# Expert layer 2: the softmax exponential of the router as a power on GpSimd, the ranking of experts two to three tiles later

## What is computed

```python
ln2_out = _layernorm(hidden_after_attn, ln2_weight, ln2_bias)
x = ln2_out.reshape(-1, H)
logits = jnp.einsum('th,eh->te', x, router_weight)          # 8 experts
gate = jax.nn.softmax(logits, axis=-1)
top_probs, top_idx = jax.lax.top_k(gate, TOP_K)             # 2 of 8
h_mid = jax.nn.gelu(jnp.einsum('th,ehf->etf', x, moe_w1))   # 128 -> 256
expert_out = jnp.einsum('etf,efh->eth', h_mid, moe_w2)      # 256 -> 128
weights = jnp.sum(jnp.where(top_idx[None] == e_ids, top_probs[None], 0.0), axis=-1)
moe_out = jnp.einsum('eth,et->th', expert_out, weights)
return hidden_after_attn + moe_out
```

## Time and profile before

| | |
|---|---|
| median of 3 runs | 976.86 us (973.74 to 979.7) |
| the profiled execution | 979.73 us |
| its span, first to last instruction | 978.0 us |
| TensorE matmul busy | 783.1 us, 80% |
| VectorE busy | 689.6 us, 71% |
| ScalarE busy | 429.1 us, 44% |
| GpSimd busy | 220.6 us, 23% |
| mean granted TensorE clock | 0.907 |

### The profile page before, as it was taken

One profiled execution on the slowest core, in us unless ns is written; L12 is line 12 of the kernel. 1 busy time (PEld: TensorE's weight loads), 2 busy tenths in 40 slices (PEclk: granted clock), 3 DMA queues, 4 the chain that ended last, 5 costly groups with the idle time before them and its releaser, 6 DMA issues. The chain is left out here.

```text
span 978.0 us, 28213 instructions
## 1 busy us (share of the span) xinstructions
PE 783.1 (80%) x10948; PEld 595.1 (61%) x10948; DVE 689.6 (71%) x1882; ACT 429.1 (44%) x848; POOL 220.6 (23%) x369
## 2 busy tenths in 40 slices
PE   2579888887338999999999716887875899999998
PEld 1345555554236777777777513655654688888886
DVE  4578888875547888888888537887753666666653
ACT  2122222221215666666666415665642455555553
POOL 4333333330430111111110086543200111111100
PEclk9568889999758999999999958999996899999999
DMA  3000000510100000010010000000000000000000
GB/s 91 20 19 20 19 19 11 128 27 11 22 7 18 27 26 27 26 27 27 26 27 27 18 0 2 5 4 4 4 4 2 1 12 11 11 11 11 9 11 14
DMA packets 31381, 19.20 MB, mean 20 GB/s; under 512 B 10590, under 2 KB 29740, under 8 KB 31276
## 3 DMA queue, kind: packets, MB, share of 16 engines
q1 hardware_dynamic: 28236, 16.73, 6.7%
q10 hardware_dynamic: 3040, 0.98, 0.4%
HBM read 7.22 MB, written 2.10 MB: 10 GB/s over the span
## 5 line engine op out<-in xcount | busy, mean ns | idle before, releaser
L1734 PEld LDWEIGHTS bank<-w2r,hme 128*128 128x128 f32 x1024 | 132.2, 191 | 16.3 <-ACT hme L1575 2.1
L1734 PE MATMUL bank<-w2r,hme 128*128 128x128 f32 x1024 | 135.6, 276 | 0.5 <-DVE Xq L1677 0.5
L1575 ACT ACTIVATE hme<-bank,b 128x512 f32<-128x512 f32 x128 | 86.4, 687 | 96.0 <-PE bank L97 95.9
L833 DVE TENSOR_SCALAR bank<-bank 128x512 f32<-128x512 f32 x128 | 88.9, 695 | 28.7 <-PE bank L904 28.7
L1677 DVE SCALAR_TENSOR_TENSOR Xq<-bank,wgte,Xq 128x128 f32 (+1 forms) x256 | 72.1, 344 | 51.1 <-PE bank L1734 38.1
L754 ACT ACTIVATE P<-bank 128x512 f32<-128x512 f32 x128 | 76.7, 599 | 66.6 <-PE bank L913 66.4
L841 DVE TENSOR_REDUCE mx<-bank 128x4 f32<-128x512 f32 x128 | 87.1, 681 | 2.1 <-PE bank L896 2.1
L350 ACT ACTIVATE sg<-bank 128x512 f32<-128x512 f32 x40 | 23.9, 597 | 127.8 <-PE bank L581 94.0
L913 PE MATMUL bank<-mT,negsel 128*128 128x128 f16 x512 | 50.1, 220 | 16.8 <-DVE bank L833 12.7
L896 PE MATMUL bank<-K,Q 128*128 128x128 f16 x512 | 51.1, 224 | 11.9 <-issue 6.5
L728 POOL TENSOR_TENSOR inv_sum<-inv_sum,dn 128x16 f32<-128x16 f32 x32 | 7.0, 220 | 230.4 <-DVE dn L872 230.4
(11 more groups left out here) (387 smaller groups left out, 2076.0 us busy)
## 6 DMA issues: line engine op xcount, KB each, us to landing
K<-Kc SPq DMA_DIRECT2D x128, 32.0 KB, 1.8
X<-in_x SPq DMA_DIRECT2D x8, 256.0 KB, 2.9
Xq<-X SPq DMA_DIRECT2D x32, 64.0 KB
Yq<-Y SPq DMA_DIRECT2D x32, 64.0 KB
out_x<-Xq SPq DMA_DIRECT2D x32, 64.0 KB, 1.7
cload<-in_ctx SPq DMA_DIRECT2D x8, 192.0 KB, 2.6
w1r<-in_L_ffn_moe_w SPq DMA_DIRECT2D x1, 1024.0 KB
w_raw<-in_L_ffn_w_gate ACTq DMA_DIRECT2D x1, 256.0 KB, 3.3
```

The lines of the kernel that those rows point to most:

```text
L833: dve.tensor_scalar(TB[j % 2][:], TB[j % 2][:], -CLIP, CLIP, ALU.max, ALU.min).then_inc(s["t_clip"], 1)
L1575: act.activation(hm[:, p % HR], UP[p % RING][:], ACT.Gelu_apprx_tanh, bias=b1[:, p:p + 1]).then_inc(s["gelu"], 1)
L1734: last = pe.matmul(Y[e % 2][:, cols], hm[:, p % HR, cols], w2r[:, p], start=(p % 2 == 0 and i == 0), stop=(p % 2 == 1), skip_group_check=True)
```

## The change

The exponential of the router moves from ScalarE to GpSimd, as a power with base e, from a new constant tile `euler`. GpSimd's residual addition goes from p = 9 to p = 5, in front of it. VectorE's three later pieces go from p = 11, 12, 13 and 14 to p = 13, 14 and 15, the last two of them joined.

```diff
+        euler = sb("euler", [128, GB, NE])
 ...
             @block.gpsimd
                 pool.memset(half[:], -0.5)
+                pool.memset(euler[:], 2.718281828459045)
 ...
-                        if nxt(g) and p == 9:
+                        if nxt(g) and p == 5:
                             pool.tensor_tensor(xg(X3, g + 1), xg(X3, g + 1), xg(H, g + 1), ALU.add
                                                ).then_inc(s["r_ready"], 1)
+                        if nxt(g) and p == 10:
+                            pool.wait_ge(s["g_in"], g + 2)
+                            pool.tensor_tensor(pr[:], euler[:], lg[:], ALU.pow).then_inc(s["g_exp"], 1)
 ...
             @block.scalar
-                        if nxt(g) and p == 10:
-                            act.wait_ge(s["g_in"], g + 2)
-                            act.activation(pr[:].rearrange("p b e -> p (b e)"), lg[:].rearrange("p b e -> p (b e)"),
-                                           ACT.Exp).then_inc(s["g_exp"], 1)
 ...
             @block.vector
-                    elif p == 11:
+                    elif p == 13:
                         dve.wait_ge(s["g_exp"], g + 1)
 ...
-                    elif p == 12:
+                    elif p == 14:
                         other = pr[:].unsqueeze(2).broadcast_to(deep)
 ...
-                    elif p == 13:
+                    elif p == 15:
                         tie = before8[:].unsqueeze(1).broadcast_to(deep)
 ...
-                    elif p == 14:
                         link(g, dve.tensor_reduce(cnt[:], c8[:, 1], AX.X, ALU.add))
```

## The result

The changed kernel took 984.91 us (median of 12 runs, 981.48 to 989.52) against 979.37 us for the kernel before (12 runs, 973.74 to 985.4): ratio 1.0055, 95% interval 1.003 to 1.008, that is 5.4 us more, with an interval of 2.9 to 7.8. The forecast was 6.8 us more. The profiled execution took 985.67 us, with a span of 984.0.

The account below looks back on a forecast made before the run. TensorE was taken to bound the loop, and VectorE's chain the start. A 5.3 us pause, 1.5 us of lower clock and 0 for the loop made 6.8 us on a median of 976.86: 983.7 us, range 979.5 to 991.

Parts of the forecast that it names:

- What bounds the kernel: Expert stage: only TensorE's stream sets the loop's time; at the start the chain runs through the exponential and VectorE.
- The 2.1 us of weight loads: Downward product's weight loads waiting for ScalarE's gelu: taken as absorbed by the matmul queue, gain 0, at most 2.1 us.
- The price: GpSimd's new 32-element power: 5.44 us, from the -0.5 power of equal size; bounds 0.22 and 6.0 us.
- The line through the shorter powers: Upper bound on the GpSimd power's length, by the slope of the 4- and 8-element powers: 6.0 us.
- The start: In step(-1) VectorE's sum comes 5.27 us later, so TensorE stands still 5.3 us for the second group's xn.
- can't begin: Step(-1): VectorE can't begin the second group's preparation before finishing the first group's routing weights, so its delay delays the end.
- The clock: TensorE's clock falls to 1.2 GHz in the start's pause; 2.9 us at half speed lose 1.5, bounds 0 and 2.9.
- The loop: Inside the loop VectorE's pieces come 1.0 us later, 0.3 us of reserve remain before TensorE's product; cost 0.
- The rival of a stalled loop: TensorE waits at p = 4 each turn if the power costs 6 us or more; about 986 to 992, chance 0.22.
- The port: Rival: GpSimd's long power holds up VectorE's combine, near 3 us in each of 7 groups; about 1005, chance 0.04.
- the `combine` that the prediction set against it: Evidence against the port rival: combine at 820.97 took its usual 1.13 us over a GpSimd power of 1.02 us.
- The sum: Whole kernel: 5.3 + 1.5 + 0 = 6.8 us more, 983.7 us against the median of 976.86, +0.7%.

Follow-up runs that it names:

- e1: Changed kernel with only the first group's exponential back on ScalarE, the other seven still powers on GpSimd; ratio to the kernel before 0.9986.
- e5: Changed kernel with all eight exponentials on ScalarE, keeping VectorE's later ranking and GpSimd's addition at p = 5; ratio to the kernel before 1.0025.
- e2: Changed kernel with 20 unused matmuls on TensorE before its wait for the second group's xn, filling the pause; ratio to the kernel before 1.0053.
- e8: Changed kernel with the first group's ranking pieces moved behind the second group's statistics on VectorE, p = 15 behind xn; ratio to the kernel before 1.0011.
- e3: Changed kernel with VectorE's pieces left at p = 11, 12, 13 and 14 as before the change; ratio to the kernel before 1.0169.
- e4: e1 with an unused 4-element power on GpSimd in front of each of the seven powers; ratio to the kernel before 1.0041.
- e7: e1 with an unused 8-element power on GpSimd in front of each of the seven powers; ratio to the kernel before 1.0058.
- e9: e1 plus 12 filler matmuls in TensorE's first xn wait and first group's p = 15 behind second group's statistics; 976.03 us, ratio to kernel before 0.9959.

## Why the prediction was right, by its steps

**What bounds the kernel.** Right: TensorE in the loop, VectorE's chain at the start. e1 and e5 show it from both sides, since neither seven exponentials on ScalarE nor seven powers on GpSimd change a turn by 0.01 us. The 2.1 us of weight loads that waited for gelu were worth nothing.

**The price.** I took 5.44 us by the row of the same shape; measured 5437 to 5438 ns, all eight. The line through the shorter powers (6.0) would have been 0.6 too high. At this shape the power of e costs what that of -0.5 does (5439 ns). Of the 15 table loads one is left.

**The start.** Forecast 5.27 us; measured 5.25 at VectorE's sum and, by e2, 5.24 at TensorE. With e8 the reason is shown too: it is what stands behind the wait on VectorE. That VectorE "can't begin" the second group before it has finished the first group's weights was the order of its stream, and no need of the data: e8 begins it earlier.

**The clock.** The mechanism was right, the size small: forecast 1.5 us, from one rise, measured 1.94 in the changed kernel's profile (1.07 in e3's). This is the term that was mis-sized. The sum took half of 2.9 us, the unbroken work at 1.2 GHz at the stage's start. After the pause the clock was 0.50 from the first work at 777.52 until 782 to 783, some 5 us. The first 1.1 us of that, the transposes, cost nothing, because the product behind them starts as late with the pause filled (16.33 us behind the bias addition in e2, 16.32 here), where it waits for `Xq`; half of the other 4.0 is the term. The Trainium skill (TensorE: Matmul & The Clock Gate, Part 1) has an idle array put back to 1.2 GHz and 2.4 GHz given again only after sustained work; the fall to 0.50 within the idle stretch and the late rise agree with it. Timed runs could not show the term.

**The loop.** Forecast: pieces 1.0 us later and 0.3 us of reserve left, at no cost. Measured 1.0 us later, 26.17 us a turn, and a reserve of 0.42 (e4) and 0.41 (e7). The predicted reserve was 0.1 short; its use as a threshold held. The rival of a stalled loop would have come true with a power of over 5.9 us (5.44 + 0.42); e4, whose power ends as late as one of 6.4 us would, is that case, at 0.57 a turn.

**The port.** Out: `combine` takes 344 ns by the median and 352 at most in the changed kernel, where two of each turn (813.33 and 816.39) run beside a power, and in e8 addition, statistics and aggregation (0.69, 0.87, 0.38 us) run under it at their usual length. The Trainium skill's warning (GPSIMD Engine Reference, 8, Key points) speaks of VectorE's instructions in a two-port mode or with two inputs in SBUF. `combine` takes the bank from PSUM, so these rows don't test it, nor did the `combine` that the prediction set against it. In e8 an instruction with two inputs in SBUF runs beside GpSimd's root, also a power. It keeps its 0.19 us, and the same holds for the comparisons behind it:

```profile
766.98 1.01 POOL L1552 TENSOR_TENSOR rs<-rs,half 128x4 f32<-128x4 f32 x1
```

```profile
767.08 0.19 DVE L1621 TENSOR_TENSOR pr<-pr,r 128x32 f32<-128x32 f32 x1
```

**The sum.** 6.8 forecast, 7.18 by the profile's stage, 5.4 (2.9 to 7.8) by time. The difference between the last two is inside what timing can tell. The absolute 983.7 us came near the measured 984.91 with some luck: it stood on a median of 976.86 from three runs, which was 979.37 over twelve, so a start 2.5 us too low and an addition 1.4 us too high cancelled in part.

## To carry to other kernels

Price an operation that changes engine at the place where nothing covers it: in a loop with a hand-written order that is the first turn, where eight equal operations had one payer. Where an in-order engine waits longer for a new producer, look at what stands behind the wait and whether it needs the result; moving one addition and its statistics ahead of it took away three quarters of the loss (5.44 of 7.18 us). A pause of the matmul engine costs its length and then some of the work behind it at 1.2 GHz, a sum that one profile with filler separates.

## What the hardware showed beyond that

One of VectorE's shortest instructions was held up by GpSimd after all, by its addition and not by its power. In e9 the copy into `wgt`, 0.18 us elsewhere, stands beside GpSimd's residual addition, and takes 1.23 us, about as long as that runs; VectorE's timeline, then GpSimd's:

```profile
767.20 1.23 DVE L1638 COPY wgte<-sele 128x32 f32<-128x32 f32 x1
768.46 1.11 DVE L1658 TENSOR_SCALAR xn<-X,mv,rs 128x128 f32<-128x128 f32 x4
```

```profile
767.12 1.27 POOL L1554 TENSOR_TENSOR Xq<-Xq,X 128x512 f32<-128x512 f32 x1
```

The long `xn` of the earlier trace rows had shown the same, 1290 ns in place of 334. Both instructions read one tensor in SBUF and write one there, and the copy ends with the addition (768.43 and 768.39). In e9 `xn` stands behind the addition, and its four take 1.11 us in place of 2.05, which bears the reading out; the mechanism is inferred from these times alone. The hold cost nothing here, for TensorE did not wait.
